# A two-layer graph kernel on one core: the second layer of each 512-row chunk moved between the big products of the next, the adjacency sums one chunk ahead, head products in fp16 pieces, the mask added by TensorE

## What is computed

```python
h = relu(layernorm(x))
# layer 0
s_left, s_right = (h @ W_sa) @ a_l, (h @ W_sa) @ a_r
e = where(adj != 0, exp(-leaky_relu(s_left[:, None] + s_right[None, :], 0.01)), 0)
x_a = (e / (e.sum(1) + 1e-5)) @ (h @ W_sa)
x_b = adj @ (h @ W_gcnb) + b_gcnb
gate_a, gate_b = sigmoid([adj @ h, h] @ Wa.T + ba), sigmoid([adj @ h, h] @ Wb.T + bb)
x = x + sigmoid(gate_a * x_a + gate_b * x_b)
# layer 1: attention inside 32 graphs of 64 rows each
h = relu(layernorm(x)); q, k, v = h @ Wq.T + bq, h @ Wk.T + bk, h @ Wv.T + bv
scores = (where(same_graph, q @ k.T / 16, 0) + adj + adj) * where(same_graph, 1, -1e6)
x = x + (softmax(scores) * same_graph) @ v
```

## Time and profile before

| | |
|---|---|
| device time, median of 3 runs | 261.23 us (260.64 to 261.25) |
| span of the profiled execution | 259.7 us |
| TensorE busy | 238.0 us (92%) |
| VectorE busy | 199.2 us (77%) |
| ScalarE busy | 149.0 us (57%) |
| GpSimd busy | 33.4 us (13%) |
| mean granted TensorE clock | 0.980 |

### The profile page before, as it was taken

One profiled execution on the slowest core, in us unless ns is written; L12 is line 12 of the kernel. 1 busy time (PEld: TensorE's weight loads), 2 busy tenths in 40 slices (PEclk: granted clock), 3 DMA queues, 4 the chain that ended last, 5 costly groups with the idle time before them and its releaser, 6 DMA issues.

```text
span 259.7 us, 5927 instructions
## 1 busy us (share of the span) xinstructions
PE 238.0 (92%) x1861; PEld 207.9 (80%) x1861; DVE 199.2 (77%) x521; ACT 149.0 (57%) x316; POOL 33.4 (13%) x29
## 2 busy tenths in 40 slices
PE   0539999999999999999999999999999899999982
PEld 0428988987888888888888888888888789999970
DVE  1796975548999849879889698898794498778883
ACT  1614673546887659533786614895331676777751
POOL 4580250000000000007000026000070001000000
PEclk9986999999999999999999999999999999999997
DMA  6999109930000492002970020000020001111111
GB/s 201 328 355 385 65 2 357 373 83 0 4 0 3 151 393 105 0 4 86 356 288 0 0 81 0 0 0 0 0 80 1 0 0 44 40 40 40 40 61 67
DMA packets 19966, 26.19 MB, mean 101 GB/s; under 512 B 1900, under 2 KB 11628, under 8 KB 19948
## 3 DMA queue, kind: packets, MB, share of 16 engines
q1 hardware_dynamic: 18800, 25.43, 27.7%
q10 hardware_dynamic: 1148, 0.53, 0.9%
HBM read 23.86 MB, written 2.10 MB: 100 GB/s over the span
## 4 chain that ended last, share of the span: by engine, by line
PE 81%; DVE 8%; ACT 3%; issue 2%; POOL 0%; DVEq 0%; ACTq 0%
PE bank L844 22%; PE bank L861 11%; PE bank L863 11%; PE bank L859 11%; PE bank L786 5%; PE bank L926 4%; PE bank L912 4%; PE bank L743 4%; PE bank L935 2%; PE bank L944 2%; DVE e_lo L1061 2%; PE bank L903 1%; DVE st L1012 1%; ACT adjt L520 1%; PE bank L920 1%
## 5 line engine op out<-in xcount | busy, mean ns | idle before, releaser
L861 PE MATMUL bank<-hd,e_hi 128*128 128x257 f16 x256 | 70.2, 274 | 0.0
L859 PE MATMUL bank<-hd,e_hi 128*128 128x257 f16 x256 | 69.7, 272 | 0.0
L863 PE MATMUL bank<-hd,e_lo 128*128 128x257 f16 x256 | 69.4, 271 | 0.0
L844 PE MATMUL bank<-hb,adjt 128*128 128x259 f16 (+1 forms) x512 | 59.0, 273 | 0.0
L844 PEld LDWEIGHTS bank<-hb,adjt 128*128 128x128 bf16 x512 | 49.7, 97 | 7.6 <-issue 0.4
L606 ACT ACTIVATE e_hi<-e_mask 128x1024 f16<-128x1024 f32 x32 | 33.8, 1059 | 35.3 <-DVE e_mask L1141 31.1
L1148 DVE SCALAR_TENSOR_TENSOR e_lo<-e_mask,e_hi 128x1024 f16<-128x1024 f32 x32 | 40.6, 1297 | 3.2 <-ACT e_hi L606 2.9
L596 ACT ACTIVATE e_raw<-s_row,nbias 128x512 f32 (+1 forms) x64 | 40.8, 707 | 1.2 <-issue 0.7
L1141 DVE SCALAR_TENSOR_TENSOR e_mask<-e_raw,adjt 128x1024 f32<-128x1024 f32 x32 | 37.9, 1222 | 4.4 <-ACT e_raw L596 3.3
L863 PEld LDWEIGHTS bank<-hd,e_lo 128*128 128x128 f16 x256 | 25.2, 98 | 3.3
L859 PEld LDWEIGHTS bank<-hd,e_hi 128*128 128x128 f16 x256 | 24.5, 96 | 3.9
(11 more groups left out here) (136 smaller groups left out, 340.2 us busy)
## 6 DMA issues: line engine op xcount, KB each, us to landing
adjt<-in_adj_t SPq DMA_DIRECT2D x16, 1024.0 KB, 10.6
adjt<-in_x SPq DMA_DIRECT2D x4, 512.0 KB, 8.0
x_in<-in_x SPq DMA_DIRECT2D x4, 512.0 KB, 3.5
out<-e_mask SPq DMA_DIRECT2D x16, 128.0 KB, 1.7
diag<-in_adj SPq DMA_DIRECT2D x16, 64.0 KB, 3.5
w_sa<-in_L_gnn_W_sa ACTq DMA_DIRECT2D x1, 256.0 KB, 4.7
w_b<-in_L_gnn_W_gcnb SPq DMA_DIRECT2D x1, 256.0 KB, 5.0
e_mask<-in_L_gnn_Wq SPq DMA_DIRECT2D x1, 256.0 KB, 7.3
```

What stands on the lines that cost most here:

```text
L844: mm = eng.matmul(bank[4 + r][:, 0:cols], adjt_b[:, bass.ds(2 * word + 1, P, 2)], hb16[:, j, part, 0:cols], start=(j == 0 and part == 0), ...
L859: eng.matmul(bank[r][:, 0:D + 1], high, hd16[:, j, 0, 0:D + 1], start=(j == 0), stop=False, skip_group_check=True)
L861: eng.matmul(bank[r][:, 0:D + 1], high, hd16[:, j, 1, 0:D + 1], start=False, stop=False, skip_group_check=True)
L863: mm = eng.matmul(bank[r][:, 0:D + 1], low, hd16[:, j, 0, 0:D + 1], start=False, stop=(j == NT - 1), skip_group_check=True)
```

## The change

1. **Layer 1 a chunk behind, four tiles a step.** Chunk k (0 to 3) has eight steps q, one for each pair of source tiles. In step q TensorE does the 24 e products of that pair (`attend`), 16 adjacency products of chunk k+1 (`sums`), and, as `beside` puts them, parts of layer 1 of chunk k-1 in four places: transposes in q=3, values in q=4, keys in q=5, scores in q=6, probabilities in q=7 and q=0 of the next chunk. After chunk 3 a round with neither e products nor sums does layer 1 of chunk 3 alone. ScalarE and VectorE have the same eight steps, each with one pair made ahead (`raw(g+4)`, `high(g+3)`; `mask(g+4)`, `low(g+3)`), then the part of layer 0 or 1 of chunk k-1 that belongs to the step. Loops are written out.
2. **Adjacency sums a chunk ahead.** Chunk 0's 128 products stand in the head, between the weight products. The sums have 71 more columns in the bank: two small products for each tile with one-hot graph classes give the counts that `counts` turns into layer 1's terms for rows outside the graph (11 VectorE instructions in step q=2, for each chunk).
3. **Head products in fp16.** hT, `w_b` and `w_sa` are scaled and split into two fp16 pieces, and each fp32 product becomes three fp16 ones. s_left is spread by products with a replicated weight column. All seven norms come from one matmul and one GpSimd power of seven columns. Graph numbers come from VectorE (`graphs`), not from GpSimd.
4. **The mask added by TensorE.** Two one-hot products (`z_same`, `z_other`, and twice adj through `ident_2`) add mask and edge terms into the scores' bank; the VectorE operations on mask, `fac` and `diag` are gone. x for the residual is loaded once into `x1_all`; ScalarE adds the 0.5 that GpSimd added (L487).

```diff
+            def sums(k, r, j):
+                if j == 0:
+                    wait(eng, b_kept, CT * k + r - 1)
...
+                for part in range(2):
+                    cols = D + 3 - part
+                    eng.matmul(B[:, r % 2, 0:cols], adjt_block(k, j, r), hb16[:, j, part, 0:cols],
...
+            def beside(k, q, place):
+                p = k - 1
...
+                if q == 0 and place in (0, 1) and p >= 1:
+                    gather(p - 1, 2 + place)
+                if q == 3 and place in (0, 2):
+                    turn_h1(p, place // 2)
+                if q == 4:
+                    values(p, place)
+                if q == 5 and place in (0, 2):
+                    keys(p, place // 2)
+                if q == 6 and place == 0:
+                    scores(p)
+                if q == 7 and place == 0:
+                    turn_p(p)
+                if q == 7 and place in (2, 3):
+                    gather(p, place - 2)
```

TensorE's loop over the chunks, and its last round:

```diff
+            for k in range(NC):
+                for q in range(NQ):
+                    for half in range(2):
+                        beside(k, q, 2 * half)
+                        if q > 0 or k == 0:
+                            attend(k, 2 * q + half)
+                        beside(k, q, 2 * half + 1)
+                        if k + 1 < NC:
+                            for j in range(8 * (q % 2) + 4 * half, 8 * (q % 2) + 4 * half + 4):
+                                sums(k + 1, q // 2, j)
+                    if q == 0 and k > 0:
+                        attend(k, 0)
+                        attend(k, 1)
+            for q in range(NQ):
+                for place in range(4):
+                    beside(NC, q, place)
```

VectorE's loop (`denominators(p)` waits for all e products of chunk p; `add_mix` also makes the new statistics), and the place of ScalarE's relu, `normalize`, which waits for `nb_all`:

```diff
+            for k in range(NC + 1):
+                p = k - 1
+                for q in range(NQ):
+                    g = NQ * k + q
+                    if q == 0 and p >= 0:
+                        denominators(p)
+                    if g + RING < PAIRS:
+                        mask(g + RING)
+                    if g + RING - 1 < PAIRS:
+                        low(g + RING - 1)
+                    if q == 0:
...
+                        if p >= 1:
+                            results(p - 1, 2)
+                            results(p - 1, 3)
+                        if 0 < k < NC:
+                            keep_b(k, 3)
+                        if p >= 0:
+                            mix(p)
+                    if q == 1:
+                        if k < NC:
+                            gate_sums(k)
+                        if p >= 0:
+                            add_mix(p)
+                    if q == 2:
+                        if k < NC:
+                            gates_out(k)
+                            counts(k)
+                        if p >= 0:
+                            shifts(p)
...
+                        if q == 2:
+                            normalize(p)
```

More of the change, by code:

```diff
@@ L790, in bias_product @@
[L790 to L798 removed]
+            eng.wait_ge(sq_made, 3)
@@ new lines, in _ @@
+            eng.wait_ge(rows_kept, NC)
+            for k in range(NC):
+                for q in range(NQ):
[10 more added lines that the diff above has]
+                        attend(k, 1)
@@ L1380, in _ @@
+            results(NC - 1, 2)
+            results(NC - 1, 3)
             with if_general(eng):
```

1720 lines of the change are left out of this document (888 added, 832 removed).

## The result

The changed kernel takes 311.79 us, median of 4 runs (310.96 to 312.97), where the kernel before took 261.1 beside it: a ratio of 1.195, 95% interval 1.192 to 1.198. The change costs 50 us. The profiled execution's span is 309.1 us (before 259.7).

What follows compares the result with a forecast made beforehand. TensorE's own pace was taken to bound the chunks, with waits deciding the change. Head 18.7 + 53.4, chunks 39.5 + 54.9 + 56.6 + 49.1 and last round 35.7 gave a 307.9 us span, so 309 us; range 284 to 325.

Steps and rivals of the forecast that it cites:

- start of the head: Up to the first weight product: it starts at 18.7 us (today 19.22), bounds 16 and 21, gate columns landing at 9.3.
- rest of the head: First weight product to first e product: 44.3 us of TensorE work plus waits of 6.4, 0.7 and 2.0, together 53.4.
- chunk 1: Transposes start 20.6 us after the last e product, then 32.3 of work and 2.0 of slow clock: 54.9 us.
- chunk 2: Chain of 22.3 us to the transposes, then 32.3 of work and 2.0 of slow clock: 56.6 us.
- chunk 3: No sums to do; chain of 22.3 us, 24.3 of work, 2.0 clock, 0.5 for the probabilities: 49.1 us.
- last round: Layer 1 of chunk 3 with nothing beside it: 35.7 us, TensorE busy for about 15.
- Waits in the chunks: TensorE idles before the first transposes of chunks 1 to 3, until relu and `nb_all`: some 6, 7 and 12 us.
- Work behind the transposes: In chunks 1 and 2, TensorE's work from the transposes to the last e product: 32.3 us.
- Clock: After each long wait TensorE runs at half clock for a while: 2.0 us charged a stall, bounds 0 to 4.
- TensorE's whole work: Over the whole kernel, TensorE's work falls by 3 us of 230.
- Rival (a): The shift is in time, so chunks 1 and 2 have neither stall nor slow clock: 278 us; chance 13%.
- Rival (b): TensorE never waits and the kernel gets faster: 258 us; chance 4%.

Runs made afterwards that it cites:

- b_cmp_late: The kernel before the change, with GpSimd's comparison of 2048 numbers waiting until VectorE has made the scaled weights: 257.31 us, ratio 0.985.
- a_shift_first: The changed kernel with VectorE's counts behind the shift instead of ahead of it in step q=2: 305.42 us, ratio 1.170.
- a_keep_clock: The changed kernel with 166 useless TensorE products in the waits before the first transposes of layer 1 of chunks 0, 1 and 2: 306.08 us.
- a_one_start: The changed kernel with each chunk's score products ordered by kind and a start flag on the first mask product alone: 306.52 us, ratio 1.174.
- a_best_clock: a_best2 with 76 useless TensorE products ahead of the last round's wait for relu: 300.66 us, ratio 1.152.
- a_chain_first: The changed kernel with mix, tanh, add_mix, shift and relu ahead of the pairs in ScalarE's and VectorE's lists: 300.75 us, ratio 1.150.
- a_best2: The changed kernel with awaited work ahead of pairs in each step, scores by kind with one start flag, graph numbers later in the head: 294.81 us.

## Why the prediction was right

The forecast was 309 us and the result 311.8, inside its own range. The mechanism was right: each of chunks 1 to 3 and the last round has one long wait, before the first transposes, released by relu, and that by `nb_all`. The sizes were less good than the total: waits were put too long and work too short, and that the two cancel is luck. The terms one by one (boundaries at 20.5, 72.7, 113.1, 167.3, 224.1 and 271.8 us of the changed kernel's span of 309.1):

| term | predicted | measured |
|---|---|---|
| start of the head | 18.7 | 20.5 |
| rest of the head | 53.4 | 52.2 |
| chunk 0 | 39.5 | 40.4 |
| chunk 1 | 54.9 | 54.2 |
| chunk 2 | 56.6 | 56.8 |
| chunk 3 | 49.1 | 47.7 |
| last round | 35.7 | 37.3 |

- **Start of the head.** Missed by 1.8, for the squares waited for the gate columns until 11.9 us (10.6 to 12.0 in the ten kernels with this order) and not 9.3. The removed comparison did make VectorE's reductions short (0.42 us each), as b_cmp_late shows by itself; in this change the gain was spent on the wait for transfers and on relu, transposes and the norm product behind them.
- **Rest of the head.** Right within 1.2, but made otherwise. Its end at 72.7 is where the key weights' products begin; the first e product, which the prediction put at 72.1, came at 74.5. TensorE's waits are 3.9 us (52.20 - 48.35) where 9.1 were predicted. The third weight product came 9.2 us behind the first, near the predicted 10.0, but only 2.11 us of that are a wait, for relu at 25.38. The rest is the clock, which the sum left out here: up to 29.5 us products start 0.22 us apart and behind it 0.11, and that cost some 3 us (an estimate, 31 products of 0.1 each).
- **Waits in the chunks.** Predicted 6.4, 7 and 12, measured 4.8, 4.9 and 10.3. The chain was mis-sized: in chunk 1 the transposes began 132.37 - 113.1 = 19.3 us behind the last e product and not 20.6, spread over its steps, in chunks 2 and 3 20.7 and 20.8 and not 22.3. TensorE's own work until q=3 was 14.5, not 14.2. That GpSimd's power is hidden under the counts held by 1.2 us only (a_shift_first).
- **Work behind the transposes.** Predicted 32.3, measured 33.8 to the last e product at full clock (a_keep_clock; 34.8 to `den`, which waits 1 us more): layer 1's pieces take 12.1 us of it where I had 10.9. The scores are most of that: 3.3 us for an estimated 2.25, since the changes of kind and of rows cost 0.25 us a tile (a_one_start). The too short work and the too long wait cancel within 1.4 us in each chunk.
- **Clock.** Predicted 2.0 a stall; measured 1.1, 2.3, 0.45 net and, in the last round, 2.7 (from the transposes to the scores 294.65 - 282.70 = 11.95 us, in a_best_clock 9.25). The order of size held, a constant did not. By the Trainium skill (TensorE: Matmul & The Clock Gate, "HAM oscillation — how this bites in real kernels") each such gap puts the engine back to half clock: all four waits agree, with 0.50 in the first 2 us behind those of chunks 1 and 2.
- **Last round.** 1.6 too short, 1.1 of it the scores. TensorE is busy for 20.3 us of it and not for about 15.
- **TensorE's whole work** was to fall by 3 us (the terms that the prediction lists add up to 2), and its busy time rose by 12.1. That was wrong in its sign. The slow clock is some 10 of it and the scores 4, by the figures above.
- **Rival (a)** put the time at 278 if the shift is in time. a_chain_first makes that true for chunks 1 and 2 and takes 300.75. Chunks 1 and 2 are 4.6 and 4.4 us above the rival's price, 1.7 each by work and the rest by waits of v and h1T that it left out. Chunk 3 is 10.2 us above it (44.8 for 34.6), for there the shift came 11.5 us behind the last e product and not within 9. Rival (b), faster, fails more clearly still: with most waits removed (a_best2) TensorE is busy for 245.2 us, not 3 less than 238, and idle for 48.6.

## What to carry to other kernels

Work that is interleaved into a stream bound by TensorE should find what it waits for ahead of work made in advance in the lists of the other engines: the order alone was worth 14 us here (311.8 to 297.6). Four pairs of buffers ahead buy nothing for a chain that queues behind the filling of them. A software pipeline over tiles that becomes steps of four tiles has to pay its whole latency once at the end, here 35 us, with nothing beside it. Before re-building a kernel, look for one instruction that takes nine times what its like takes: one line there gave 3.8 us, the re-building cost 50.
